# Moving the split of six routed experts' weights from the tile stage into the attention stage

## The reference

```python
x = x + tanh(g_xattn[1]) * attention(layernorm(x), ctx, ctx, mask, Wq, Wk, Wv, Wo)   # 16 heads, 4 key groups, ALiBi
x = x + tanh(g_ffn[1]) * moe(layernorm(x))

def moe(x):                      # 2048 tokens, 8 experts, 352 inner, top 2 of 8
    combine = top2_softmax(x @ router_w.T)
    for e in range(8):
        acc += combine[:, e] * ((silu(x @ gate_w[e]) * (x @ up_w[e])) @ down_w[e])
    return acc + (silu(x @ s_gate_w + s_gate_b) * (x @ s_up_w + s_up_b)) @ s_down_w + s_down_b
```

## Time and profile before

| | |
|---|---|
| runs | 1140.69, 1141.89, 1152.41 us (median 1141.89) |
| profiled execution, first to last instruction | 1146.9 us |
| mean granted TensorE clock | 0.962 of full speed |
| PE busy | 1028.8 us, 90% |
| DVE busy | 747.0 us, 65% |
| ACT busy | 601.8 us, 52% |
| POOL busy | 456.0 us, 40% |
| chain that ended last: PE in the tile stage | L2578 6%, L2565 12% of the span |
| POOL waits for `rec` in attention (L1332) | 184.0 us in 15 waits |

### The profile page before, as it was taken

How to read it: one execution, slowest core, us unless ns; L and a number is a source line. 1 busy time by engine, 2 the same in 40 slices (tenths; PEclk the granted TensorE clock), 3 DMA queues, 4 the chain that set the end, 5 groups by cost and what they waited for, 6 DMA issues and landing times. The chain is left out here.

```text
span 1146.9 us, 17729 instructions
## 1 busy us (share of the span) xinstructions
PE 1028.8 (90%) x5438; PEld 475.5 (41%) x5439; DVE 747.0 (65%) x1419; ACT 601.8 (52%) x898; POOL 456.0 (40%) x483
## 2 busy tenths in 40 slices
PE   0466889999789999999999998999998899999996
PEld 0243445555423223323322324455445455555542
DVE  6988988888786776578477547745545344443347
ACT  6897999999346776467467565452211111111110
POOL 1100335544410242243134341000657788889065
PEclk9978899999979999999999999998999899999998
DMA  9322930000534234134211004201678888976588
GB/s 325 114 74 80 342 138 1 2 1 9 133 89 107 80 82 116 62 58 94 66 48 44 12 21 136 76 26 52 243 282 170 200 205 207 206 192 146 153 284 291
DMA packets 174204, 142.39 MB, mean 124 GB/s; under 512 B 121364, under 2 KB 137108, under 8 KB 173624
## 3 DMA queue, kind: packets, MB, share of 16 engines
q1 hardware_dynamic: 163560, 110.40, 34.7%
q0 software_dynamic: 8672, 29.76, 7.9%
q10 hardware_dynamic: 1904, 1.38, 0.6%
HBM read 70.93 MB, written 43.37 MB: 100 GB/s over the span
## 5 line engine op out<-in xcount | busy, mean ns | idle before, releaser
L1432 ACT ACTIVATE prob<-p_col,mask_col,any_key 128x512 f32<-128x512 f32 x256 | 186.2, 781 | 103.2 <-PE p_col L1564 102.3
L1653 DVE CUSTOM_DVE_ANT_0 ajunk<-p_row,mask_row 128x512 bf16<-128x512 f32 x256 | 166.2, 686 | 64.1 <-PE p_row L1513 62.5
L1526 PE MATMUL p_out<-prob,v 128*64 128x512 f32 x512 | 138.1, 618 | 0.1
L1332 POOL TENSOR_TENSOR o<-sum_a,rec 32x512 f32<-32x512 f32 x30 | 39.1, 1304 | 186.1 <-DMA rec<-inv_d 184.0
L1513 PE MATMUL p_row<-ks,early_place 99*128 99x512 f16 x256 | 100.5, 395 | 8.7 <-DVE top L1653 8.0
L1564 PE MATMUL p_col<-early_place,ks 101*128 101x512 f16 x256 | 97.7, 385 | 0.9 <-ACT prob L1432 0.3
L2647 DVE SCALAR_TENSOR_TENSOR shid<-s_up,ssilu 128x352 f32<-128x352 f32 x39 | 20.4, 524 | 99.0 <-PE s_up L2565 98.8
L2513 ACT ACTIVATE ssilu<-s_gate 128x352 f32<-128x352 f32 x39 | 18.1, 463 | 124.0 <-PE s_gate L2565 124.0
L2578 PE MATMUL s_down<-mw,shT 128*128 (+1 forms) x351 | 82.0, 379 | 0.0
L2565 PE MATMUL s_gate<-mw,sxT 128*128 x444 | 74.1, 318 | 6.7 <-DMA sxT<-x_slots 6.7
L2565 PE MATMUL s_up<-mw,sxT 128*128 x444 | 73.5, 316 | 0.0
(11 more groups left out here) (354 smaller groups left out, 2077.3 us busy)
## 6 DMA issues: line engine op xcount, KB each, us to landing
x_slots<-nought SPq DMA_DIRECT2D x3, 3328.0 KB, 18.4
y_slots<-y SPq DMA_DIRECT2D x39, 256.0 KB, 2.2
early_place<-in_ctx SPq DMA_DIRECT2D x8, 1024.0 KB, 6.2
early_place<-halves_d SPq DMA_DIRECT2D x45, 128.0 KB, 2.5
halves_d<-halves SPq DMA_DIRECT2D x18, 256.0 KB, 2.1
mstg<-in_L_ffn_gate_w POOLq DMA_DIRECT2D x6, 704.0 KB, 5.7
mstg<-in_L_ffn_up_w POOLq DMA_DIRECT2D x6, 704.0 KB, 6.0
x<-in_x SPq DMA_DIRECT2D x4, 1024.0 KB, 7.3
```

The source lines that it names most:

```text
L1432: nc.scalar.activation(prob[s % 4][:, c, :], p_col[c][:], ACT.Exp, bias=mask_col[:, b, k:k + 1], scale=any_key[:, b:b + 1]).then_inc(t_exp, 1)
L1526: mm = nc.tensor.matmul(p_out[pr][c * 2 * DH:(c + 1) * 2 * DH, :], v1[b % 2][:, k, g, :], prob[n % 4][:, c, :], start=(k == 0), stop=(k == ...
L1653: nc.vector.tensor_tensor_reduce(junk[:, n % 2, :], p_row[n % 2][:], mask_row[:, blk // HPG, :], 1.0, -3e38, ALU.add, ALU.max, top[blk % 2 ...
```

## The change

Three things are changed. In attention, POOL splits experts 2 to 7 part by part: two part buffers for float32 and one for both halves lie in the weight buffer `wst`, which is free once its own weights have been split. Per part it waits for the load and for the store of the part before, converts and scales (two TENSOR_SCALAR), subtracts, stores both halves to `split_d` in DRAM, and issues the load of the part after next. `PARTS_AT` gives how many parts follow behind `normalise(blk - 2)` of each block. In the tile stage POOL only issues six loads of 128 x 8704 float16, two in flight, and a semaphore `e_have` counts the experts that are there. Four tiles instead of two are turned at the end of `stage_shared`, so that SP's loads in the tile stage start with tiles 4 and 5. Since these four fill all of `keep`, ACT's loads of the first shared weights move from behind tile 3 to behind tile 29.

```diff
+    PARTS_AT = (3, 3, 2, 2, 1, 2, 2, 2, 1, 2, 2, 2, 0, 0, 0, 0, 0)
...
+            stage = [wst[:, n * KB * EI:(n + 1) * KB * EI] for n in range(2)]
+            both = wst[:, 2 * KB * EI:3 * KB * EI].bitcast(F16).rearrange("p (h c) -> p h c", h=2)
...
+            def split_expert(c):
+
+                e, q = parts[c]
+                at, n, _ = W_PARTS[q]
+                w32 = stage[q % 2][:, 0:n]
+                pool.wait_ge(t_ew[q % 2], 16 * (c // 2 + 1))
+                need(pool, t_ed, 16 * c)
+                pool.nop(nofuse=True)
+                nc.gpsimd.tensor_scalar(both[:, 0, 0:n], w32, W_UP, 0.0, ALU.mult, ALU.add).then_inc(t_eh, 1)
+                nc.gpsimd.tensor_scalar(w32, w32, W_UP, 0.0, ALU.mult, ALU.add).then_inc(t_es, 1)
+                pool.wait_ge(t_eh, c + 1)
+                pool.wait_ge(t_es, c + 1)
+                pool.nop(nofuse=True)
+                nc.gpsimd.tensor_tensor(both[:, 1, 0:n], w32, both[:, 0, 0:n], ALU.subtract).then_inc(t_el, 1)
+                pool.wait_ge(t_el, c + 1)
+                pool.nop(nofuse=True)
+                nc.gpsimd.dma_start(split_d[e - EARLY, :, :, at:at + n], both[:, :, 0:n]).then_inc(t_ed, 16)
+                if c + 2 < len(parts):
+                    load_expert(c + 2)
+
+            pool.wait_ge(t_split, KB + 1)
+            load_expert(0)
+            load_expert(1)
+            done_parts = 0
             for blk in range(BLOCKS + 1):
                 if blk > 1:
                     normalise(blk - 2)
                 if blk % HPG == HPG - 1 and blk < BLOCKS - 1:
                     ln_power(blk // HPG + 2)
+                for c in range(done_parts, done_parts + PARTS_AT[blk]):
+                    split_expert(c)
+                done_parts += PARTS_AT[blk]
+            pool.wait_ge(t_ed, 16 * len(parts))
...
+FIRST = 4
...
-            for n in range(2):
+            for n in range(FIRST):
                 sp.dma_start_transpose(first_xT[:, n].rearrange("p h k t -> p (h k) t"), x_slots[n * P:(n + 1) * P, :]).then_inc(m_first[n], 16)
...
             for n in range(2):
-                load(2 + n, n)
+                load(FIRST + n, n)
...
-            load(EARLY, 0)
-            load(EARLY, 1)
-            with pool.Fori(EARLY, EXPERTS - 1) as e:
-                split(e, True)
-            split(EXPERTS - 1, False)
+            for e in range(EARLY):
+                pool.nop(nofuse=True).then_inc(e_have, 1)
+
+            for e in range(EARLY, EXPERTS):
+                if e >= EARLY + 2:
+                    pool.wait_ge(e_w[e % 2], 16 * (e // 2 - EARLY // 2))
+                    pool.nop(nofuse=True).then_inc(e_have, 1)
+                nc.gpsimd.dma_start(w[:, 2 * e * WC:2 * (e + 1) * WC], split_d[e - EARLY].rearrange("p h c -> p (h c)")).then_inc(e_w[e % 2], 16)
...
-                pe.wait_ge(m_wl, NQ * e + (NQ * 3 + MORE))
+                pe.wait_ge(e_have, e + 1)
```

More of the change, by code:

```diff
@@ L1138, in stage_attention @@
     FIRST = 16 * 3 * 2
+    PARTS_AT = (3, 3, 2, 2, 1, 2, 2, 2, 1, 2, 2, 2, 0, 0, 0, 0, 0)
+    assert len(PARTS_AT) == BLOCKS + 1 and sum(PARTS_AT) == (EXPERTS - EARLY) * len(W_PARTS)
     def copied(eng, f):
@@ L1341, in normalise, with load_expert @@
                 nc.gpsimd.tensor_tensor(oT[1][:, j, :], o[:], oT[0][:, j, :], ALU.subtract).then_inc(t_ol, 1)
+            t_ew = (t_ew0, t_ew1)
+            parts = [(e, q) for e in range(EARLY, EXPERTS) for q in range(len(W_PARTS))]
+            stage = [wst[:, n * KB * EI:(n + 1) * KB * EI] for n in range(2)]
+            both = wst[:, 2 * KB * EI:3 * KB * EI].bitcast(F16).rearrange("p (h c) -> p h c", h=2)
+            def load_expert(c):
+                e, q = parts[c]
+                load_part(nc.gpsimd, stage, t_ew, q, *(a["L1_ffn_" + t][e] for t in ("gate_w", "up_w", "down_w")))
+            def split_expert(c):
+                e, q = parts[c]
+                at, n, _ = W_PARTS[q]
[18 more added lines that the diff above has]
+            done_parts = 0
             for blk in range(BLOCKS + 1):
@@ L2358, in stage_tiles @@
     names = ("const", "xina", "xinb", "gate", "up", "silu", "hid", "hh", "hl", "hta", "htb", "down", "y", "sta", "stb",
-             "ga", "gb", "gc", "sum", "out", "pool", "wa", "wb", "dve", "pre", "lu", "lv", "ld0", "ld1", "bd")
+             "ga", "gb", "gc", "sum", "out", "pool", "wa", "wb", "dve", "pre", "lu", "lv", "ld0", "ld1", "bd", "have")
     (e_const, e_xina, e_xinb, e_gate, e_up, e_silu, e_hid, e_hh, e_hl, e_hta, e_htb, e_down, e_y, e_sta, e_stb,
-     e_ga, e_gb, e_gc, e_sum, e_out, e_pool, e_wa, e_wb, e_dve, e_pre, e_lu, e_lv, e_ld0, e_ld1, e_bd) = (sem("e_" + n) for n in names)
+     e_ga, e_gb, e_gc, e_sum, e_out, e_pool, e_wa, e_wb, e_dve, e_pre, e_lu, e_lv, e_ld0, e_ld1, e_bd, e_have) = (sem("e_" + n) for n in names)
     e_w = (e_wa, e_wb)
@@ L2368, in stage_tiles @@
     PAIRS_OF_TILES = TILES // 2
+    LATE_LOADS_AT = PAIRS_OF_TILES - 4
     def tile_of(t, i):
@@ L2384, in first, with ahead @@
         return isinstance(r, int) and r == 0
-    def last(r):
-        return isinstance(r, int) and r == PAIRS_OF_TILES
+    def ahead(r):
+        return isinstance(r, int) and 2 * r < FIRST
     with nc.Block() as block:
@@ L2423, in body @@
                     store(r - 1, n)
-            for n in range(2):
-                body(0, n, False)
-            with sp.Fori(1, PAIRS_OF_TILES - 1) as r:
+            for r in range(FIRST // 2):
+                for n in range(2):
+                    body(r, n, False)
+            with sp.Fori(FIRST // 2, PAIRS_OF_TILES - 1) as r:
                 for n in range(2):
@@ L2493, in _ @@
+            for e in range(EXPERTS - 2, EXPERTS):
+                pool.wait_ge(e_w[e % 2], 16 * (e // 2 - EARLY // 2 + 1))
+                pool.nop(nofuse=True).then_inc(e_have, 1)
             for t in range(NT):
@@ L2522, in _ @@
                     body(r, n)
-            act.wait_ge(e_up, 2)
+            with act.Fori(2, LATE_LOADS_AT) as r:
+                for n in range(2):
+                    body(r, n)
             nc.scalar.dma_start(first_gate, shared_d[0, :, :, G0:U0]).then_inc(e_pre, 16)
@@ L2584, in body @@
                 e = expert(i)
-                pe.wait_ge(*((m_first[n], 16) if first(r) else (e_xin[n], 16 * r)))
-                pe.wait_ge(m_wl, NQ * e + (NQ * 3 + MORE))
+                pe.wait_ge(*((m_first[i], 16) if ahead(r) else (e_xin[n], 16 * (r - (FIRST // 2 - 1)))))
+                pe.wait_ge(e_have, e + 1)
                 product(r, n, e, G0, p_gate, e_gate, e_silu)
```

60 lines of the change are left out of this document (17 added, 43 removed).

## The result

| | before | changed |
|---|---|---|
| runs, median (lowest to highest), us | 1141.89 (1140.69 to 1152.41) | 1253.26 (1241.18 to 1261.02) |
| profiled execution, us | 1146.9 | 1239.1 |
| first load of the shared expert's stage, us | 691.3 | 739.9 |
| first matmul of the tile stage, us | 860.6 | 909.5 |
| tile stage to the end, us | 286.3 | 329.6 |

The changed kernel takes 1.087 times as long, 95% interval 1.081 to 1.093; this ratio takes executions in the faster of the device's two states only (the one of 1261.02 us was not), so it isn't the ratio of the medians. The direction was predicted, the size wasn't: 1174 stood in the prediction and 1194 was the end of its range. The table splits the 92.2 us by which the two profiled executions differ: 48.6 are lost before the shared stage, 0.3 in it, and 43.3 in the tile stage, of which the sum had expected a gain of 7.4.

The account below looks back on a forecast made before the run. PE bounds attention, so POOL's late parts make PE wait. 1146.9 + 36.0 (lateness) + 2 + 2 + 2 (smaller terms) - 9.4 (removed stop) = 1179.5; the median lies 5.0 lower: 1174 us, range 1131 to 1194.

Parts of the forecast that it names:

- the sum: Whole kernel: 1146.9 + 36.0 + 2 + 2 + 2 - 9.4 = 1179.5 us against the profiled execution.
- PE bounds attention, and what makes it wait is paid in full: Attention: PE works 49.85 of 50 us, so anything that makes PE wait is added to the time.
- The start of POOL's work: Attention: first load there at 345.6, six parts with five waits, normalise(0) starts at 402.5, its multiplications end at 408.2.
- Who waits: Attention: ACT waits for late POOL ahead of its block 2 copy, delaying PE through the exponentials; later blocks tested likewise.
- How much: Attention: POOL's lateness costs 12.8 us at block 2 and 36.0 us in all by normalise(10).
- its list of signs: Attention: an ACT wait for POOL over 8 us ahead of the third copy into sum_a, with five smaller ones.
- DVE slowed by POOL, 2 us, and the transfers, nothing at all: Attention: some 22 us of DVE slowing mostly hidden by its waits for PE, 2 us counted; no transfer term.
- the DVE term: Attention: DVE slowed beside POOL's arithmetic, taken as 2 us, with 0 and 22 as ends.
- two small terms of 2: DVE slowed beside POOL in attention, 2 us, and PE's matmuls running slow after long stops, 2 us.
- The give-back of 9.4 us: Tile stage: removing the 6.37 us stop ahead of tile 5 and slow matmuls after it returns the full 9.4 us.
- Burst: Tile stage rival, chance 0.10: six chained loads delay transposes for tiles 6 to 11, 3.8 us each, +23 us.

Follow-up runs that it names:

- the arithmetic alone: Kernel before plus the changed attention stage, without the parts' DMAs and their waits; attention copies 334.9 us, 12.7 more than before, total 1161.56 us.
- the transfers alone: Kernel before plus the changed attention stage, parts' loads and stores only, no operations; attention copies 358.4 us, 36.2 more than before, total 1181.22 us.
- the order alone: Kernel before with only four tiles turned ahead and ACT's shared-weight loads behind tile 29, no split in attention; 1145.66 us, ratio 1.002.

## Why the prediction was right or wrong, step by step

The profiled execution is 59.6 us longer than the 1179.5 of the sum: 50.7 of them in the tile stage, where the sum had -7.4 and +43.3 came, 8.6 in attention (48.6 for 40) and 0.3 in the shared stage.

- **PE bounds attention, and what makes it wait is paid in full**: right. PE's busy time fell from 49.85 to 42.89 in 50 us.
- **The start of POOL's work**: predicted 345.6 for the first scaling, 402.5 for `normalise(0)`, 408.2 for the end of its multiplications.

```profile
348.12 1.37 POOL L1364 TENSOR_SCALAR early_place<-early_place 128x1408 f16<-128x1408 f32 x1 [3.37 <-DMA early_place<-in_L_ffn_gate_w]
...
384.31 0.61 POOL L1364 TENSOR_SCALAR early_place<-early_place 128x512 f16<-128x512 f32 x1 [6.73 <-issue]
...
407.73 1.38 POOL L1336 TENSOR_TENSOR o<-sum_a,rec 32x512 f32<-32x512 f32 x1
```

  2.5, 5.2 and 5.1 us later. The 704 KB stores land in 3.9 us in the median where I took 4.5; the estimate by the Trainium skill (DMA: Bandwidth & Descriptors, Anatomy of one DMA), 3.7, was nearer. But a median wasn't what counted: the first six stores took 5.1, 4.5, 8.1, 2.4, 4.0 and 3.5 us. All of POOL's five waits between the six parts end when a store lands, and they make 17.6 us (3.81, 3.33, 6.73, 1.10 and 2.67) where the sum had 11.8. The 6.73 us above are the store of 512 KB, issued at 376.07, for which I had put 3.7 from issue to landing and a wait of 2.1. The operations themselves were 3.1 us shorter than reckoned, which hides half of it.
- **Who waits**: ACT ahead of its copies in blocks 2, 3, 4, 7, 8, 11 and 12, and these seven alone, as the sum lists them (its list of signs has one large wait and five smaller ones, one too few). **How much**: 36.0 predicted, 19.2 measured. The longest was to be over 8 us and was 4.8:

```profile
413.41 0.58 ACT L1453 COPY sum_a<-p_out 128x512 f32<-128x512 f32 x1 [4.61 <-POOL o L1336]
...
463.04 0.58 ACT L1453 COPY sum_a<-p_out 128x512 f32<-128x512 f32 x1 [4.75 <-POOL o L1336]
```

  The copy of block 2 would have come at 408.8 without this wait and not at 394.43, since blocks 0 and 1 and PE's other waits had used up 14 us already. The lateness was real, and was partly hidden under losses that the sum had at almost nothing.
- **DVE slowed by POOL, 2 us, and the transfers, nothing at all**: this step failed. With no lateness in play the arithmetic alone costs 12.7 us and the transfers alone 36.2; in the changed kernel the two, overlapping with each other and with the lateness, are the 29 above, if the lateness is taken at its own length. The ends of the DVE term (0 and 22) held the value and my choice in them was poor: I let DVE's wait for PE cover it, but `topb`, at 387 and 700 ns, stands on the way from the maxima to the next block. For the transfers there was no term. I asked when POOL's DMAs land and never what lands late beside them: SP's groups of transposes, and the 8 KB of denominators.
- **Attention in sum**: 36 and two small terms of 2 against 48.6. The total is nearer than its parts: the lateness came out at half, the two terms for DVE and the transfers at many times what I had, and that they nearly cancel is luck.
- **The give-back of 9.4 us**: failed. The stop went, as said, but the order alone brought 284.2 against 286.3 us in the stage, and no change in the total that is clear of noise (ratio 0.9994 to 1.0047). Taking the latest arrival away lets the next latest one decide; I had credited the whole distance.
- **Burst, chance 0.10, +23 us**: this was the second cause, and it measured +43.3. Its price was 3.8 us for each of six tiles, from one load that took 11.3 us; in the event one transpose held PE for 40.81 us. The sum itself had no term for it, and that is the step that failed in the tile stage. The sentence that kept it small, that large rows move cheaply, is the one the runs turn round: at 17,408 bytes a row PE waits 48.8 us, at 2,176 bytes 11.6. I also looked for it at the token tiles 6 to 11 (`sxT`) and not at the hidden rows of tile 0 (`shT`), which nothing can turn ahead.

Two corrections, each measured, lead to the kernel that loads one at a time: attention at 48.6 in place of 40, and its tile stage at 288.0 - 286.3 = +1.7 in place of -7.4 make 1174.5 + 8.6 + 9.1 = 1192; it took 1195.29. The second correction comes from that same run, so this checks only that nothing else of size is left over. What the changed kernel takes beyond that is the burst.

## What to carry to other kernels

Ask of every large DMA that is moved or merged not only when it lands but what small, many-piece transfer is issued beside it, above all a transpose of something computed just before: PE waits for that one, and no prefetch can cover it. Ask the same of every small load on which an engine waits in the order of its list, as DVE does for the denominators. In this kernel large loads at such a place cost least one at a time with pauses between them, and less in short rows than in long ones; check the size of the stop rather than the bandwidth. And credit a removed stop only down to the next latest arrival.

## What the hardware showed that I had not expected

- A DMA transpose of hidden rows, issued beside loads with rows of 17,408 bytes, two in flight, kept the issuing queue for 10.51 us and landed after 46.0, the next for 22.50 and after 51.5, where 1.21 and 2.7 were usual; in that time both queues together moved down to 28 GB/s in some slices. The first landed in 21.9 us at 8,704 bytes, 13.1 at 2,176, and 5.7 with one load at a time.
- Loads of 24 parts cost 13.9 us and stores 4.9, and both together 36.2. Whether two kinds together do it, or only that they fall on other moments, no run separates: ten parts of both kinds cost 1.3 us where they missed the transposes and 23.0 where they met them.
- An 8 KB load from SP landed in 6.2 and 6.4 us beside POOL's 704 KB transfers, where it took 2.5 at most before.
- GpSimd slowed even VectorE's smallest operations: a cast of 128x16 went from 274 to 387 ns on average with arithmetic beside it, and to 744 in the changed kernel. The Trainium skill (GPSIMD Engine Reference, Specifications) names the shared interface, and as the operations concerned those with two SBUF inputs or in a two-port mode. The cast has one input; whether it runs in a two-port mode the trace doesn't show.
- The granted clock was 1.00 (the level of 2.4 GHz) when PE stopped at 922, and 0.50 (the level of 1.2) from 931 to 966, PE doing nothing until 962.93; the 0.73 and 0.72 of the two windows above are averages over both levels. From 1000 on it was 1.00; the down product right after the stop took 4.02 us where 1.94 is its time at 1.00. With the gate behind it (2.29 for 1.79) the first stop costs 2.6 us more than PE's wait says.
